# Six x jobs of 512 tokens, K and Q in the tail, inverses and spread one slot later, and all turned probabilities copied by ScalarE

## The reference

```python
q, k, v = heads(x @ Wq + bq), heads(x @ Wk + bk), heads(x @ Wv + bv)
scores = einsum('bhqd,bhkd->bhqk', q, k) / sqrt(64)
probs = softmax(scores + where(adj, 0.0, -9e15))
ctx = einsum('bhqk,bhkd->bhqd', probs, v)      # heads joined again: 8 x 1024 x 384
y = x + (ctx @ Wf + bf)
out = (y - mean(y)) / sqrt(var(y) + 1e-5)      # over the features
```

## Time and profile before

| what | value |
|---|---|
| median of three runs | 1580.09 us (1570.0 to 1587.43) |
| the profiled execution | 1580.77 us, its span 1578.5 us |
| TensorE busy | 1484.5 us, 94% of the span |
| VectorE busy | 880.2 us, 56% |
| ScalarE busy | 878.3 us, 56% |
| GpSimd busy | 376.7 us, 24% |
| mean granted TensorE clock | 0.994 |

### The profile page before, as it was taken

One profiled execution on the slowest core, in us unless ns is written; L12 is line 12 of the kernel. 1 busy time (PEld: TensorE's weight loads), 2 busy tenths in 40 slices (PEclk: granted clock), 3 DMA queues, 4 the chain that ended last, 5 costly groups with the idle time before them and its releaser, 6 DMA issues.

```text
span 1578.5 us, 31676 instructions
## 1 busy us (share of the span) xinstructions
PE 1484.5 (94%) x11088; PEld 1142.6 (72%) x11088; DVE 880.2 (56%) x1688; ACT 878.3 (56%) x1653; POOL 376.7 (24%) x676
## 2 busy tenths in 40 slices
PE   7999899999999999999999999999999999999995
PEld 6777677776877767776777776877677776777664
DVE  5566545655456655555555564555545565455553
ACT  4666535666366653666536665366644666446562
POOL 0222232121322213222133221332212322123222
PEclk9999999999999999999999999999999999999998
DMA  3021110211002111121101221012110021001111
GB/s 123 15 58 29 24 30 15 58 28 28 26 18 55 28 28 26 18 58 28 25 26 18 58 28 28 26 17 56 28 28 26 18 68 28 14 24 18 28 21 27
DMA packets 95540, 51.41 MB, mean 33 GB/s; under 512 B 56704, under 2 KB 95360, under 8 KB 95360
## 3 DMA queue, kind: packets, MB, share of 16 engines
q1 hardware_dynamic: 95360, 49.12, 13.1%
HBM read 36.31 MB, written 12.78 MB: 31 GB/s over the span
## 4 chain that ended last, share of the span: by engine, by line
PE 64%; DMA 14%; issue 9%; ACT 6%; DVE 4%; SPq 3%; DVEq 1%; POOL 0%; ACTq 0%; POOLq 0%
PE score_ps L434 15%; PE turn_ps L447 13%; PE context_ps L460 13%; DMA spread_dram<-inv_sum 12%; ACT prob L548 4%; PE misc_ps L347 4%; PE misc_ps L349 4%; PE misc_ps L348 4%; PE score_ps L347 2%; PE score_ps L349 2%; PE score_ps L348 2%; PE misc_ps L355 1%; SPq L305 1%; DMA inv_rows<-spread_dram 1%; DVE prob L651 1%
## 5 line engine op out<-in xcount | busy, mean ns | idle before, releaser
L548 ACT ACTIVATE prob<-prob,row_min 128x1024 f32<-128x1024 f32 x384 | 440.0, 1146 | 506.4 <-DVE row_min L651 489.5
L651 DVE CUSTOM_DVE_ANT_0 prob<-score_ps,mask 128x1024 f32<-128x1024 f32 x384 | 454.9, 1222 | 255.7 <-PE score_ps L434 229.8
L447 PE MATMUL turn_ps<-ident,prob 128*128 128x128 f32 x3072 | 414.4, 277 | 33.1 <-ACT prob_t L557 23.9
L447 PEld LDWEIGHTS turn_ps<-ident,prob 128*128 128x128 f32 x3072 | 337.1, 140 | 130.6 <-issue 77.5
L460 PE MATMUL context_ps<-prob_t,v_all 128*64 128x256 f32 x3072 | 372.9, 386 | 0.8 <-ACT prob_t L557 0.8
L796 POOL TENSOR_TENSOR context_lo<-context,context_hi 128x256 fp32r<-128x256 f32 x96 | 70.5, 735 | 1034.7 <-ACT context_hi L571 1034.7
L460 PEld LDWEIGHTS context_ps<-prob_t,v_all 128*64 128x64 f32 x3072 | 205.0, 137 | 145.9 <-issue 61.2
L557 ACT ACTIVATE prob_t<-turn_ps 128x512 f32<-128x512 f32 x384 | 224.5, 585 | 46.6 <-PE turn_ps L447 45.9
L660 DVE COPY prob_t<-turn_ps 128x512 f32<-128x512 f32 x192 | 132.5, 690 | 32.4 <-PE turn_ps L447 31.3
L434 PE MATMUL score_ps<-k_hi,q_hi 64*128 64x512 f32 x768 | 141.3, 446 | 5.6 <-issue 4.6
L434 PE MATMUL score_ps<-k_lo,q_hi 64*128 64x512 f32 x768 | 120.8, 391 | 0.0
(11 more groups left out here) (85 smaller groups left out, 1774.6 us busy)
## 6 DMA issues: line engine op xcount, KB each, us to landing
x_in<-in_x_dram SPq DMA_DIRECT2D x32, 384.0 KB, 5.5
inv_rows<-spread_dram SPq DMA_DIRECT2D x192, 64.0 KB, 3.9
out_dram<-res SPq DMA_DIRECT2D x32, 384.0 KB, 2.8
adj_in<-in_adj_dram SPq DMA_DIRECT2D x64, 128.0 KB, 3.4
spread_dram<-inv_sum SPq DMA_DIRECT2D x96, 2.0 KB
prob_t<-in_L_gnn_Wk_dram SPq DMA_DIRECT2D x1, 576.0 KB, 4.3
prob_t<-in_L_gnn_Wq_dram SPq DMA_DIRECT2D x1, 576.0 KB, 7.1
prob_t<-in_L_gnn_Wv_dram SPq DMA_DIRECT2D x1, 576.0 KB, 8.5
```

Source lines behind the costliest of these rows:

```text
L447: last = pe.transpose(turn_ps[:, half, i, :], prob[:, u % 4, kt * P:(kt + 1) * P], ident[:])
L548: nc.scalar.activation(prob[:, t % 4, :], prob[:, t % 4, :], ACT.Exp, scale=-1.0, bias=row_min[:, t % 4:t % 4 + 1], accum_out=row_sum[:, t ...
L651: nc.vector.tensor_tensor_reduce(prob[:, t % 4, :], score_ps[:, t % 2, :], mask[:, qt, :], 1.0, HUGE, ALU.add, ALU.min, row_min[:, t % 4:t ...
```

## The change

- x of the next batch is transposed in six jobs of one feature block and 512 tokens (four transposes each) in place of eight jobs of 128 tokens and three blocks. They stand in slots 7, 13, 19, 20, 21 and 22, between the turns. There are no END jobs any more.
- ("k", 0, 0) and ("q", 0, 0) of the next batch leave slots 21 and 22 and become the first and the seventh of nine TAIL jobs.
- Two V jobs (`AHEAD`) are run in slots 1 and 2 ahead of the first turn, into `context_ps`; the other V jobs follow in slots 1 and 2, and all q jobs up to ("q", 2, 1) come one slot earlier. The mix always stands before the first turn of its slot.
- The next x is loaded in four pieces in slots 3, 5, 7 and 9; the residual adds move from slots 4 to 7 to slots 1 to 4.
- ScalarE copies both banks of every unit, and does so before the exponential that stood ahead of them. VectorE's `copy_even_second` is gone.
- `denominators(p)` moves from the end of slot 2p+1 to slot 2p+2 (behind its masks), and `spread(p)` from slot 2p+1 to slot 2p+2 of SP's queue, behind an adjacency load where the slot has one. The last pair's stand behind the last slot.

```diff
-MID_NEXT = {19: ("x", 1, 0), 20: ("x", 3, 0), 21: ("k", 0, 0), 22: ("q", 0, 0)}
-END = {1: ("v", 5, 0)}
-END_NEXT = {18: ("x", 0, 0), 19: ("x", 2, 0), 20: ("x", 4, 0), 21: ("x", 5, 0), 22: ("x", 6, 0), 23: ("x", 7, 0)}
-TAIL = (("k", 0, 1), ("k", 1, 0), ("k", 1, 1), ("k", 2, 0), ("k", 2, 1), ("q", 1, 0), ("q", 2, 0))
+AHEAD = {1: ("v", 4, 0), 2: ("v", 6, 0)}
+MID = {1: ("v", 5, 0), 2: ("v", 7, 0), 3: ("q", 0, 1), 4: ("q", 1, 1), 6: ("q", 2, 1), 8: ("q", 0, 2), 9: ("p", 0, 0),
+       10: ("q", 1, 2), 11: ("p", 1, 0), 12: ("q", 2, 2), 14: ("q", 0, 3), 15: ("p", 2, 0), 16: ("q", 1, 3),
+       17: ("p", 3, 0), 18: ("q", 2, 3), 23: ("p", 4, 0)}
+MID_NEXT = dict(zip((7, 13, 19, 20, 21, 22), x_jobs()))
+TAIL = tuple([("k", pair, half) for pair in range(3) for half in range(2)] + [("q", pair, 0) for pair in range(3)])
...
 # SP, body of a batch
                 for s in range(SLOTS):
                     if s % 6 >= 4 and (s // 6 < 2 or with_next):
                         load_adjacency(b, s // 6 + 1, s % 6 - 4)
-                    if s % 2 == 1:
-                        spread(b, s // 2)
-                    if s == 9 and with_next:
-                        sp.wait_ge(res_done, b * TT + TT)
-                        load_x(b + 1)
+                    if s % 2 == 0 and s:
+                        spread(b, s // 2 - 1)
+                    if s in (3, 5, 7, 9) and with_next:
+                        g = (s - 3) // 2
+                        sp.wait_ge(res_done, b * TT + (2 * g + 2))
+                        load_x(b + 1, g)
                     if s in (13, 19):
                         store(b, (s - 13) // 6)
+                spread(b, PAIRS - 1)
                 store(b, 2)
                 store(b, 3)
...
 # TensorE, a slot
-                    if mid and mixing:
-                        mix(b, *mixing)
+                    if s in AHEAD:
+                        ahead(b, AHEAD[s], with_next)
+                    if mixing:
+                        mix(b, *mixing)
                     turn(b, 2 * s - 2)
                     if mid:
                         misc(b, mid, with_next)
-                    elif mixing:
-                        mix(b, *mixing)
                     turn(b, 2 * s - 1)
-                    if end:
-                        misc(b, end, with_next)
...
 # ScalarE, a slot
-                    exponential(b, 2 * s)
                     if s:
                         copy_first(b, 2 * s - 2)
-                    exponential(b, 2 * s + 1)
+                        copy_second(b, 2 * s - 2)
+                    exponential(b, 2 * s)
                     if mixing and mixing[1] == 1:
                         context_high(b, mixing[0])
-                    if mid and mid[0] in "qkx":
-                        high_part(b, mid)
+                    if mid and mid[0] in "qx":
+                        high_part(b, mid, with_next)
                     if s:
                         copy_first(b, 2 * s - 1)
-                        copy_odd_second(b, 2 * s - 1)
-                    if end and end[0] == "x":
-                        high_part(b, end)
+                        copy_second(b, 2 * s - 1)
+                    exponential(b, 2 * s + 1)
...
 # VectorE, a slot and the end of a batch
+                    if s % 2 == 0:
+                        denominators(b, s // 2 - 1)
                     if mixing and mixing[1] == 1:
                         divide(b, mixing[0])
-                    copy_even_second(b, 2 * s - 2)
...
-                    if s % 2 == 1:
-                        denominators(b, s // 2)
...
                 divide(b, PAIRS - 2)
-                copy_even_second(b, UNITS - 2)
+                denominators(b, PAIRS - 1)
                 if with_next:
-                    low_part(b, TAIL[0])
+                    for n in range(3):
+                        low_part(b, TAIL[n], with_next)
...
                 divide(b, PAIRS - 1)
                 if with_next:
+                    low_part(b, TAIL[3], with_next)
                     add_residual(b, 5)
                     moments(b, 5)
-                    for n in range(3, 7):
-                        low_part(b, TAIL[n])
+                    for n in range(4, len(TAIL)):
+                        low_part(b, TAIL[n], with_next)
...
 # GpSimd, a slot
-                    if 4 <= s < 8:
-                        residual(b, s - 4)
+                    if 1 <= s < 5:
+                        residual(b, s - 1)
```

More of the change, by code:

```diff
@@ L90, in batch_jobs @@
     for s in range(1, SLOTS):
-        jobs += [job for job in (mid_job(s, with_next), end_job(s, with_next)) if job]
+        jobs += [job for job in (AHEAD.get(s), mid_job(s, with_next)) if job]
     return jobs + (list(TAIL) if with_next else [])
@@ L115, in graph_attention @@
     first = first_jobs()
[L116 to L120, removed]
+    start_jobs = x_jobs() + first
+    loop_jobs = {w: [j for j in batch_jobs(w) if j[0] != "p"] for w in (False, True)}
+    loop_splits = {w: [j for j in loop_jobs[w] if j[0] != "v"] for w in (False, True)}
+    off_misc = TAIL + EARLY_V[:2] + EARLY_V[3:] + tuple(AHEAD.values())
+    misc_jobs = {w: [j for j in batch_jobs(w) if j not in off_misc] + [("p", 5, 0), ("p", 6, 0)] for w in (False, True)}
     x_tiles = x.rearrange("b (t p) h -> b p t h", p=P)
@@ L233, in job_bank @@
             if b is None:
-                return score_bank((first.index(job) + 3) % 4 if job in first else job[1] % 4)
+                return score_bank(start_jobs.index(job) % 4)
             if job in TAIL:
@@ L277, in _ @@
             load_weight(1, wk)
-            load_x(0)
+            for g in range(4):
+                load_x(0, g)
             load_weight(0, wq)
@@ L400, in misc, with ahead @@
                 else:
-                    pe.wait_ge(job_out, jobs_through(b, prior))
-                if job[0] == "x" and job[1] % 2 == 0:
-                    pe.wait_ge(x_loaded[job[1] // 2], b * 16 + 32)
-                if job == ("k", 0, 0):
-                    pe.wait_ge(job_out, jobs_through(b, ("x", 3, 0)))
-                if job == ("q", 0, 0):
-                    pe.wait_ge(job_out, jobs_through(b, ("x", 1, 0)))
+                    pe.wait_ge(job_out, jobs_through(b, prior, with_next))
+                if job[0] == "x" and job[1] == 0:
+                    for g in (2 * job[2], 2 * job[2] + 1):
+                        pe.wait_ge(x_loaded[g], b * 16 + 32)
+                run(b, job)
+            def ahead(b, job, with_next):
+                pe.wait_ge(job_out, jobs_through(b, EARLY_V[1] if job == AHEAD[1] else AHEAD[1], with_next))
                 run(b, job)
@@ L425, in scores @@
                 if qt == 0 and group:
-                    pe.wait_ge(job_out, jobs_through(b, ("q", pair, group)))
+                    pe.wait_ge(job_out, jobs_through(b, ("q", pair, group), with_next))
                 q = slice(qt * P, (qt + 1) * P)
@@ L511, in _ @@
             pe.wait_ge(ident_done, 1)
-            for tile in range(TT):
-                if tile % 2 == 0:
-                    pe.wait_ge(x_loaded[tile // 2], 16)
-                if tile >= 4:
-                    pe.wait_ge(job_out, tile - 3)
-                transpose_x(None, tile)
+            for n, (kind, t, half) in enumerate(x_jobs()):
+                if t == 0:
+                    for g in (2 * half, 2 * half + 1):
+                        pe.wait_ge(x_loaded[g], 16)
+                if n >= 4:
+                    pe.wait_ge(job_out, n - 3)
+                transpose_x(None, t, half)
             for k, job in enumerate(first):
                 pe.wait_ge(weights_done, 1 if job[0] == "k" else 2)
-                pe.wait_ge(job_out, TT if k < 4 else jobs_through(None, first[k - 4]))
-                project_qk(None, *job, job[2])
+                pe.wait_ge(job_out, 3 if k == 0 else max(6, k + 3))
+                project_qk(None, *job)
             pe.wait_ge(weights_done, 4)
@@ L764, in _ @@
                     dve.wait_ge(bias_scaled, 2)
[L765 removed]
+                low_part(None, what, True)
             dve.wait_ge(vf_biases_in, 32)
```

141 lines of the change are left out of this document (63 added, 78 removed).

## The result

The changed kernel takes 1673.95 us (median of four runs, 1667.1 to 1677.19); the kernel before took 1580.39 beside it (1570.0 to 1587.43). The ratio is 1.0592, with a 95% interval of 1.0524 to 1.066: 6% slower. The forecast of 1697 lay 23 us too high, inside its range of 1634 to 1755. The profiled execution took 1674.65, its span is 1672.6.

What follows compares the result with a forecast made beforehand. TensorE bounds the kernel, busy 184.6 of 193.4 us a looping batch. Per batch 21.6 lost to late divides less 6.8 won is +14.8, times seven 104; with about 12 in the last batch, 1580.8 becomes 1697 us, range 1634 to 1755.

Steps and rivals of the forecast that it cites:

- What is won: Looping batch: x transposes' waits 4.4, turns' waits 3.6, transitions 0.3, less 1.5 lost: 6.8 us won.
- The order's loss: ScalarE's copies before the exponential: 0.1 us lost in each of ten even slots; slot 5, without a job, waits 0.5.
- the transitions': TensorE: two x jobs fewer save about 0.3 us of transitions a batch.
- The hold-up: SP's queue: spread waits behind an adjacency load, leaving at S4+11.2 for pair 1, S+9.2 for pairs 4, 7 and 10.
- The round trip: Inverse sums through DRAM, from spread's issue to the divide: 13.0 us, bounds 11.8 and 14.3.
- Pair 1: Late divide stalls TensorE 6.2 us in slot 7, low clock adds 2.5: 8.7 a batch.
- Pairs 4 and 7: Late divides stall TensorE 3.1 us each; half of the 2.5 clock price added to each, together 8.7 a batch.
- Pair 10 and the tail: Late divides in the tail: last mix 1.8 us late, fourth job's bank delays the eighth 0.4, ninth waits 1.2; together 3.4.
- Slow writes elsewhere: All other pairs: slow writes now and then pass the free time of the divide, 0.8 us a batch.
- The ends: Last batch's exposed end grows by 3.5 us, inverses standing behind divide(10); the start unchanged within 1 us.
- that rival: Hidden transfer: spread not held back or round trip short, so 6.8 a batch is won: 1531 us; chance 0.06.
- The copies' order: Rival: evictions ahead of exponentials cost 0.6 us in each even slot instead of 0.1, transfers hidden: 1571; chance 0.03.

Runs made afterwards that it cites:

- the kernel without the write: Changed kernel, SP's order kept, without the DRAM write of the inverse sums and its wait; reads fetch numbers of Wq: 1531.42 us, ratio 0.9687.
- the spread-first kernel: Changed kernel with spread ahead of the adjacency load of the same slot in SP's queue: 1542.0 us, ratio 0.9756; again on another chip 1542.81 us, 0.9774.
- the move alone: Kernel before with only the inverses and the spread moved as the change moves them: 1726.68 us, ratio 1.0913.
- the second version: Changed kernel with spread ahead of the adjacency load, x's high part behind the second turn's copies, last inverses ahead of divide(10): 1558.9 us on the slower chip, later 1534.44.
- the kernel with earlier residuals: Changed kernel with the residual adds in slots 0 to 3 in place of 1 to 4: 1651.74 us, ratio 1.0435.

## Why the prediction was right, and where it was off

**What is won.** Right in cause; the size came out near because errors cancel. The sum had 6.8 us a batch and about 2 in the last, 49 in all, and the kernel without the write has 49.2. The order's loss was put at 0.1 in each even slot and 0.5 in slot 5, some 15 us over all batches with the last's slots without a job. Without the write the mixes wait 14.4 us for copies and 7.9 in gaps of 0.2 to 0.3 behind which the profile shows no releaser, and the turns 5.5: 28. Two waits of 0.81 a batch lead, in slots 21 and 23 (in the changed kernel at 597.69 and 610.42), because x's high part is 512 wide and takes 0.60 ahead of the copies; the sum went by the 256-wide part. Against these 13, TensorE's busy time fell by 10.7 us (1484.5 in the page of before, 1473.8 without the write) where the sum had 4.6, the transitions' 2.1 and the clock's 2.5. And the last batch's exposed end, which the sum lets grow from 6.2 to 9.7, is 1.9 without a write. The kernel in which only the spread isn't held back has 38.6.

**The hold-up.** Right to the tenth: adjacency load at S4+10.7 and spread at S4+11.2 were forecast, 10.7 and 11.3 came. At pairs 4, 7 and 10 the forecast was S+9.2, and the rows have 9.4, 9.3 and 9.3 (slots 10, 16 and 22 start at 516.77, 558.31 and 602.06, the spreads leave at 526.13, 567.63 and 611.38).

**The round trip.** 13.0 was taken, with bounds of 11.8 and 14.3. In the batch shown it was 13.7 at pair 1, 11.7 at pair 4, 13.0 at pair 7 and 14.0 at pair 10; over the thirty blocked spreads the mean is 12.7 (11.1 to 14.0): the whole is nearly right, the parts aren't. From issue to the reads' issue the write took 7.7 at pair 1 and 8.2 at the median of all, where before's typical row had 9.1; the reads behind it took 6.0 to the divide at pair 1 (488.15 to 494.12), where the earlier trace rows has 3.7. A second chip had the long writes too, 9.2 at the median. But before took 1598 us there and 1580 in its own profiled execution, so whether the long writes of that profile are a chip's or that kernel's own isn't settled.

**Pair 1.** Forecast 6.2 of stall and 2.5 of clock. The eight stalls sum to 49.5, 6.2 each; the sixteen mixes and the next turn lose 1.7 and 0.6 to the clock, 2.3. Right.

**Pairs 4 and 7.** Forecast 3.1 each, and the clock's price in half of the cases. Pair 4 stalled 2.2 on the mean of eight batches (1.25 to 3.2), pair 7 3.0 of seven (2.4 to 3.7). The granted clock fell to 0.50 behind six of the seven stalls at pair 7 and three of the eight at pair 4. TensorE was busy for 32.9 us of these low stretches; half of that, 16.4, is their price, an estimate that holds the work of a low stretch to take twice its time. (By the same reckoning pair 1 cost 18.3, the tail 1.7 and the last wait 2.0, 38.4 in all, where TensorE's busy time is 39.8 above that without the write, 1513.6 against 1473.8.) Stalls of 17.7 and 21.3 and these 16.4 make 55, where the forecast had 65. Half of the cases was a fair guess for the clock; the stalls at pair 4 were shorter than forecast since the round trip was, 12.1 on the mean.

**Pair 10 and the tail.** The step that was most off for its size. Forecast 3.4 a batch, 24 in all, of which 1.8 for the last mix and 1.6 for the banks behind it. Found: the mix waits 2.26 in the batch shown, where the write took 10.6 us (611.38 to 622.02), 1.59 where it took 10.1, and 0.28 to 0.69 in the other five, where it took 7.7 to 8.2; 6.2 over the seven instead of 12.6. So the last mix is late mainly behind a slow write. The waits for k's low part are 8.7 above those of the spread-first kernel, where 11.2 were forecast. With 1.7 for one low stretch of the clock (at 644.77) that makes 17.

**Slow writes elsewhere.** Forecast 0.8 a batch, 6 in all. In the spread-first kernel, where every pair has the room that these pairs had, the mixes wait only 1.7 us longer than without the write; in the changed kernel all mixes but those of the four blocked pairs wait 14.6, as without the write. Mis-sized: the writes were shorter than in the rows of before.

**The ends.** The last wait is 8.9 instead of 6.2, 2.7 more against 3.5 forecast; the first scores start 1.4 later (30.95 against 29.52).

**The balance.** Against the kernel without the write, the 1531 of the sum before its losses, the losses came out lower by 2 us at pair 1, 10 at pairs 4 and 7, 7 in the tail and 6 for slow writes, and TensorE's waits on its own issue and at the turns are 5 lower; its last wait with its clock is 9 longer. That makes 21 of the 23 us. The range was met through the right mechanism, its middle in part by errors that cancel.

The rivals fell as the prediction had them fall. Transfers aren't hidden; with the spread not held back the time is 1542, 11 above the 1531 of that rival, which only the kernel without the write comes to. The copies' order costs 0.8 us in two slots of a batch and 0.2 to 0.3 in others, not 0.6 in ten. The Trainium skill, DMA: Bandwidth & Descriptors, section Anatomy of one DMA, gives about 2.0 us plus the bytes over 436 GB/s, fitted to DMAs that GpSimd issues; by it this write would take an estimated 2.0. SP issues the write here and no run shows such a time for it: the measured 8.2 (9.2 on the other chip) decides.

## What to carry to other kernels

A queue that issues in order turns every wait in it into a wait of everything behind it. When a latency-bound transfer is moved in such a queue, list the waits that it now stands behind, and put the one whose result is due soonest first: a load whose data is wanted some 30 us later can stand behind it for nothing, while the reverse cost 125 us on one chip here. And read a sum of gains and losses by two experiments, one without each side: the move alone (146 lost) and the change without the write (49 won) added up to the result (93.6 lost) within 4 us. Look at what else such an experiment takes away: with the spread-first kernel's 39 in place of the 49, which hold a shorter end, the sum misses by 14.

## What the runs showed of the hardware that was not expected

A write of 2 KB to DRAM in elements of 4 bytes takes 8.2 to 8.4 us at the median from its issue to the issue behind its wait on two of the chips (6.9 to 11.6), and 9.2 on a third (7.6 to 12.7). Half the elements save 0.6 to 0.7 us of the wait, less than the 1.0 between chips.

Single reads can take far longer than the median: one of 12.0 us to land was worth a stall of 7.8 us in the second version on the slower chip.

The granted clock knows two levels in these traces, 1.00 and 0.50 (2.4 and 1.2 GHz); 0.53 above is a stretch that holds both. In the changed kernel it was at 0.50 within 0.5 us of the mix's start behind each of the eight stalls at pair 1 (5.4 to 6.7 us) and behind five of 3.01 to 3.68. Behind eight stalls of 1.25 to 2.43 it stayed at full. Behind four, of 2.08, 2.70, 2.94 and 3.21, TensorE went on at full clock for 0.8 to 1.2 us first and then fell to 0.50, as here behind the one of 2.94, whose mix starts at 336.41:

```profile
336.41:337.41 1.00, 1.00 (x10) 0.73 (x12) 1.00 (x3) 0.90 (x2) 0.65 (x4) 1.00 0.00 0
337.91:339.91 2.00, 2.00 (x11) 1.23 (x8) 0.09 (x2) 0.00 (x0) 1.35 (x6) 0.50 0.00 0
```

Length alone doesn't sort them: the stall of 2.08 brought the low level and the one of 2.43 didn't, and in the kernel with earlier residuals one of 3.02 didn't either. Of the 132 us between the changed and the spread-first kernel 37 are TensorE's busy time, and so the clock, more than a quarter.
